# A two-pass attention and FFN kernel: the order of the first pair's units, the weight words' loads, and the way of the first unit's maxima are changed

## The reference, cut to what matters

```python
ig, fg = x @ Wi + bi, x @ Wf + bf                # x = [q, k, v], per head and token
log_f_cum = cumsum(log_sigmoid(fg))              # with a leading 0
log_D = where(ltr, log_f_cum[s] - log_f_cum[t], -inf) + ig[t]
max_log_D = max(log_D, -1)
D = exp(log_D - max_log_D)
C = (q @ k.T / sqrt(32)) * D
Cn = C / (maximum(abs(C.sum(-1)), exp(-max_log_D)) + EPS)
h = Cn @ v                                       # then normalised over the 32 features of a head
x = x + h * ln_scale
gate_up = layernorm(x) @ w_gu.T                  # fp4 values times a scale per group of 128
y = (silu(gate) * up) @ w_down.T
x = x + y / rms(y)
```

## Time and profile before

| | us |
|---|---|
| median of the runs | 559.58 |
| the profiled execution | 560.9 |
| its span | 559.2 |
| TensorE matmuls busy | 504.4 |
| VectorE busy | 391.4 |
| GpSimd busy | 331.9 |
| ScalarE busy | 295.6 |

### The profile page before, as it was taken

How to read it: one execution, slowest core, us unless ns; L and a number is a source line. 1 busy time by engine, 2 the same in 40 slices (tenths; PEclk the granted TensorE clock), 3 DMA queues, 4 the chain that set the end, 5 groups by cost and what they waited for, 6 DMA issues and landing times.

```text
span 559.2 us, 8167 instructions
## 1 busy us (share of the span) xinstructions
PE 504.4 (90%) x2728; PEld 279.4 (50%) x2728; DVE 391.4 (70%) x691; ACT 295.6 (53%) x639; POOL 331.9 (59%) x371
## 2 busy tenths in 40 slices
PE   0449989968999899999999999999999989988996
PEld 0326765425666444456665445466664443322442
DVE  4675886985888897647777899377778962877301
ACT  0335765275777623377786354577766123866000
POOL 1043533457888685466777783767777662888501
PEclk9868996988999999999999999999999999999999
DMA  8654309164200600166006000653000000200000
GB/s 254 174 156 186 114 2 320 38 227 151 77 1 2 226 1 1 42 222 240 28 2 226 1 0 4 198 212 119 2 0 2 19 20 19 94 1 1 19 20 38
DMA packets 22218, 48.33 MB, mean 86 GB/s; under 512 B 1824, under 2 KB 8864, under 8 KB 21536
## 3 DMA queue, kind: packets, MB, share of 16 engines
q1 hardware_dynamic: 22176, 47.81, 25.4%
HBM read 37.84 MB, written 4.33 MB: 75 GB/s over the span
## 4 chain that ended last, share of the span: by engine, by line
PE 68%; DVE 14%; issue 5%; ACT 4%; POOL 4%; DMA 4%; SPq 1%; DVEq 0%; POOLq 0%; ACTq 0%
PE pf L972 25%; PE pf L958 17%; PE po L896 9%; PE pq L864 6%; PE pq L876 2%; DMA ts<-in_gate_up_bytes 2%; DVE ffn L1221 2%; PE pq L958 2%; PE pq L901 2%; ACT dmat L648 2%; PE pf L981 2%; DVE ffn L1225 1%; PE pq L826 1%; POOL hT L530 1%; ACT ts L682 1%
## 5 line engine op out<-in xcount | busy, mean ns | idle before, releaser
L972 PE MATMUL pf<-w_down,hT 128*128 128x512 f32 x352 | 154.1, 595 | 1.7 <-DVE w_down L1287 1.7
L958 PE MATMUL pf<-yT,gu_val 128*128 128x512 f16 x552 | 135.6, 385 | 4.2 <-ACT th L707 1.5
L525 POOL TENSOR_TENSOR ffn<-ffn,ts 128x512 f32<-128x512 f32 x88 | 117.6, 1337 | 31.9 <-DVE ffn L1225 22.1
L682 ACT ACTIVATE ts<-pf,gu_scale 128x512 f32<-128x512 f32 x138 | 87.5, 684 | 51.1 <-PE pf L958 50.8
L972 PEld LDWEIGHTS pf<-w_down,hT 128*128 128x128 f32 x352 | 65.9, 190 | 83.7 <-issue 77.1
L958 PEld LDWEIGHTS pf<-yT,gu_val 128*128 128x128 f16 x552 | 50.7, 99 | 68.7 <-DVE ffn L1225 8.2
L648 ACT ACTIVATE dmat<-negm,aT 128x128 f32<-128x128 f32 x256 | 80.0, 395 | 4.9 <-DMA negm<-negm_dram 4.9
L530 POOL TENSOR_TENSOR hT<-ffn,th 128x512 f32<-128x512 f32 x44 | 57.6, 1313 | 30.9 <-DVE th L1234 30.9
L1221 DVE SCALAR_TENSOR_TENSOR ffn<-pf,gu_scale,ts 128x512 f32<-128x512 f32 x69 | 51.6, 748 | 33.7 <-PE pf L958 20.0
L896 PEld LDWEIGHTS po<-v_sb,dmat 128*128 128x128 f32 x512 | 64.2, 197 | 5.3 <-issue 0.9
L486 POOL TENSOR_SCALAR_AFFINE_SELECT dmat<-dmat 128x512 f32<-128x512 f32 x64 | 44.2, 704 | 30.7 <-ACT dmat L648 30.7
(11 more groups left out here) (118 smaller groups left out, 634.0 us busy)
## 6 DMA issues: line engine op xcount, KB each, us to landing
negm<-negm_dram SPq DMA_DIRECT2D x32, 512.0 KB, 5.3
ffn<-in_x SPq DMA_DIRECT2D x4, 1024.0 KB, 7.5
xT<-in_ctx_T SPq DMA_DIRECT2D x16, 256.0 KB, 5.8
ctx_sb<-in_ctx SPq DMA_DIRECT2D x4, 1024.0 KB, 5.4
x_sb<-in_x SPq DMA_DIRECT2D x4, 1024.0 KB, 5.2
x_res<-x_sb SPq DMA_DIRECT2D x4, 1024.0 KB, 5.3
out<-x_res SPq DMA_DIRECT2D x16, 256.0 KB, 2.1
ts<-in_gate_up_bytes SPq DMA_DIRECT2D x2, 704.0 KB, 11.8
```

The source lines that it names most:

```text
L525: pool.tensor_tensor(acc, acc, ts[:, h % TDEEP, 1], ALU.add).then_inc(tsum_ready, 1)
L682: act.activation(ts[:, h % TDEEP, g], bank(q, h, g), ACT.Copy, scale=gu_scale[:, g * GU + o:g * GU + o + 1]).then_inc(t_ready, 1)
L958: last = pe.matmul(bank(q, h, g), gu_val[:, h // 2 + h % 2 * FT, g], yT[:, part, g], start=(part == 0), stop=(part == 1))
L972: last = pe.matmul(pf[:, tt], hT[:, j, tt * P:(tt + 1) * P], w_down[:, j], start=(j == 0), stop=(j == FT - 1))
```

## The change

Five parts.

1. The words of the up weights are loaded in two halves, the first ahead of the context (`load_gu`), and the next pair's x is loaded already in the head, behind a wait for the transposes of x, where it stands ahead of `sc_raw`. Four chunks are decoded ahead of the gate rows and none between head and units (`UP_FIRST`, `UP_EARLY`); the statistics of the next x (`norm1_sums(1)`) take that place and leave the units.
2. The maxima of unit 0 of pair 0 are spread over the partitions by TensorE (`spread_first`, four f32 matmuls with a column of the identity), into two banks of `pf`, from where ScalarE reads them. SyncE no longer loads that unit's maxima. The turned rows go to bank 0 of `pf`. 24 fillers stand ahead.
3. In pair 0 the values of the context are centred for two tiles first, then unit 0 is masked, then the other two tiles are centred; `floors` moves behind the exponentials of unit 0.
4. In pair 0 TensorE issues both halves of the scores and the state sums of u + 1 in front of the values of u, with one group of fillers; the state sums have their own bank, and VectorE's `later_part` of a unit moves behind the products of the next.
5. In pair 1 GpSimd's mask of unit 0 stands one step earlier.

```diff
--- before
+++ after
@@ -76,8 +76,8 @@
 UP_CHUNKS = 8
-UP_FIRST = 3
-UP_EARLY = 5
+UP_FIRST = 4
+UP_EARLY = 4
 DOWN_CHUNKS = 4
@@ -213,10 +213,13 @@
         def bank_back(p):
-            return pf[:, 3] if p == 1 else pm
+            return pf[:, 0] if p == 0 else pf[:, 3] if p == 1 else pm
...
             return pf[:, 2 * half] if p == 0 and u % 2 else pq[:, 2 * half]
+        def bank_state(p):
+            return pf[:, 1] if p == 0 else pq[:, 1]
@@ -360,7 +364,8 @@
                 take_wait(sp)
-                load_units(range(1))
+                if not (isinstance(p, int) and p == 0):
+                    load_units(range(1))
@@ -401,8 +406,6 @@
                     late_negm(p)
-                    if q is None:
-                        load_xg(n, q)
                     if n is not None:
@@ -415,15 +418,23 @@
+            def load_gu(part):
+                rows = slice(part * GROW // 2, (part + 1) * GROW // 2)
+                cols = slice(part * GROW * MW // 2, (part + 1) * GROW * MW // 2)
+                for half in range(2):
+                    sp.dma_start(gu_words[half * HALF:(half + 1) * HALF, rows].rearrange("p o w -> p (o w)"),
+                                 gu_bytes[:, cols]).then_inc(s_up[part], 16)
             load_xg(0, None)
...
             sp.dma_start(bias_col[:], b_gates).then_inc(s_const, 16)
+            load_gu(0)
             load_ctxT(0)
-            for half in range(2):
-                sp.dma_start(gu_words[half * HALF:(half + 1) * HALF].rearrange("p o w -> p (o w)"), gu_bytes
-                             ).then_inc(s_up, 16)
+            load_ctx(0)
+            load_gu(1)
+            load_xg(1, None)
             sp.dma_start(sc_raw[:], gu_scales).then_inc(s_scales, 16)
-            load_ctx(0)
             for half in range(2):
@@ -464,14 +475,14 @@
-            def centre_v(p):
+            def centre_v(p, tiles=range(TT)):
                 pool.wait_ge(am_ready, 2 * p + 2)
...
                     pool.wait_ge(pv_done, UNITS * p)
-                for tt in range(TT):
+                for tt in tiles:
                     m = vmean[:, 1, tt * NH:(tt + 1) * NH].unsqueeze(2).to_broadcast([P, NH, DH])
@@ -488,7 +499,9 @@
                 hg, b = u // 2, u % 2
-                if u == 0:
+                if p == 0 and u < 2:
+                    pool.wait_ge(v_ready, 2 * u + 2)
+                elif u == 0:
                     pool.wait_ge(v_ready, TT * p + TT)
@@ -546,12 +559,12 @@
                         residual2(q - 1, TT - 1)
+                    if q == 0 and h == LATE - 1:
+                        mask(p, 0)
                     if q is not None:
...
                             gated(q, h // 2 - 1)
-                    if q == 0 and h == LATE:
-                        mask(p, 0)
                     if p is not None and slot(q, h) in MASKS:
@@ -585,8 +598,9 @@
             rstd1(0)
-            centre_v(0)
+            centre_v(0, range(2))
             mask(0, 0)
+            centre_v(0, range(2, TT))
             iteration(0, None, 1)
@@ -634,8 +648,12 @@
                 hg, b = u // 2, u % 2
+                if p == 0 and u == 0:
+                    act.wait_ge(bc_done, half + 1)
+                elif half == 0:
+                    spread = 2 * p + u // 4 + 1 - (u % 4 == 0)
+                    act.wait_ge(s_negm[u % 4], 16 * spread)
                 if half == 0:
-                    act.wait_ge(s_negm[u % 4], 32 * p + 16 * (u // 4) + 16)
                     act.wait_ge(aT_ready, p + 1)
@@ -644,8 +662,9 @@
                     bh = b * DH + hg * HG + h
+                    m = pf[:, 2 * half + 1, hh * S:(hh + 1) * S] if p == 0 and u == 0 else negm[:, u % 4, h]
                     for c in range(BLKS):
-                        last = act.activation(dmat[:, u % 2, half, c, hh], negm[:, u % 4, h, c * P:(c + 1) * P],
+                        last = act.activation(dmat[:, u % 2, half, c, hh], m[:, c * P:(c + 1) * P],
                                               ACT.Exp, bias=aT[:, c, bh:bh + 1])
@@ -781,9 +800,9 @@
             softplus(0)
-            floors(0)
             exps(0, 0, 0)
             exps(0, 0, 1)
+            floors(0)
             iteration(0, None, 1)
@@ -841,7 +860,10 @@
                 hg, b = u // 2, u % 2
-                if u == 0 and hh == 0:
+                if p == 0 and u == 1 and hh == 0:
+                    pe.wait_ge(floor_ready, 2)
+                if p > 0 and u == 0 and hh == 0:
@@ -869,11 +891,14 @@
                 pe.wait_ge(vw_ready, 2 * UNITS * p + 2 * u + 2)
-                if u > 0:
+                if p == 0:
+                    if u > 0:
+                        pe.wait_ge(state_ready, u)
+                elif u > 0:
                     pe.wait_ge(later_ready, UNITS * p + u)
...
                     pe.wait_ge(t_ready, 4 * FT * q + 2)
-                pe.matmul(pq[:, 1, 0:HG * (DH + 1)], ctx_sb[:, 2 * b, hg * P:(hg + 1) * P],
+                pe.matmul(bank_state(p)[:, 0:HG * (DH + 1)], ctx_sb[:, 2 * b, hg * P:(hg + 1) * P],
                           vw[:, u % 2].rearrange("q h d -> q (h d)"), start=True, stop=True
@@ -881,7 +906,9 @@
                     pe.wait_ge(acc_ready, 4 * FT * q + 2)
-                if u == 0:
+                if p == 0 and u < 2:
+                    pe.wait_ge(v_ready, 2 * u + 2)
+                elif u == 0:
                     pe.wait_ge(v_ready, TT * p + TT)
@@ -897,6 +924,8 @@
+                if p == 0 and u > 0:
+                    pe.wait_ge(later_ready, u)
                 pe.wait_ge(state_ready, UNITS * p + u + 1)
@@ -974,11 +1003,21 @@
-            def keep_busy(count):
+            def spread_first(half):
+                if half == 0:
+                    pe.wait_ge(nm_ready, 1)
+                for hh in range(2):
+                    r = 2 * half + hh
+                    last = pe.matmul(pf[:, 2 * half + 1, hh * S:(hh + 1) * S],
+                                     ident[0:ROWS, r:r + 1].to_broadcast([ROWS, P]), nm[:], start=True, stop=True)
+                last.then_inc(bc_done, 1)
+            def keep_busy(count, dst=None):
...
                 for _ in range(count):
-                    pe.matmul(pf[:, 3], words[:, 0:P], words.unsqueeze(1).to_broadcast([P, 2, 2 * P]),
+                    pe.matmul(pf[:, 3] if dst is None else dst, words[:, 0:P], words.unsqueeze(1).to_broadcast([P, 2, 2 * P]),
                               start=True, stop=True)
@@ -990,17 +1029,15 @@
                             scores(p, q, VALUES[s] + 1, 0)
-                            keep_busy(6 if VALUES[s] == 0 else 3)
+                            state_sums(p, q, VALUES[s] + 1)
+                            scores(p, q, VALUES[s] + 1, 1)
+                            keep_busy(6, po[:]) if VALUES[s] == 0 else keep_busy(3)
                         if s in VALUES:
                             values(p, q, VALUES[s])
-                            if q is None and VALUES[s] + 1 < UNITS:
-                                scores(p, q, VALUES[s] + 1, 1)
-                                state_sums(p, q, VALUES[s] + 1)
-                                keep_busy(6 if VALUES[s] == 0 else 3)
                         if s in SCORES and (q is not None or SCORES[s] == 0):
...
                             if q is None:
-                                keep_busy(16)
+                                keep_busy(8, po[:])
                             state_sums(p, q, SCORES[s])
@@ -1027,7 +1064,10 @@
             gate_sums(0)
+            keep_busy(24, po[:])
+            spread_first(0)
             turn_back(0)
+            spread_first(1)
             iteration(0, None, 1)
@@ -1128,7 +1168,7 @@
                 dve.wait_ge(st_done, UNITS * p + u + 1)
-                dve.tensor_tensor(state[:, u % 2], pq[:, 1, 0:HG * (DH + 1)].rearrange(
+                dve.tensor_tensor(state[:, u % 2], bank_state(p)[:, 0:HG * (DH + 1)].rearrange(
                     "q (h d) -> q h d", h=HG), own_rows[:], ALU.mult).then_inc(state_ready, 1)
@@ -1265,7 +1305,9 @@
                     dve.wait_ge(const_ready, 7)
-                    dve.wait_ge(s_up, 32)
+                    dve.wait_ge(s_up[0], 32)
+                if i == UP_CHUNKS // 2:
+                    dve.wait_ge(s_up[1], 32)
                 r = slice(i // 2 * QROW, (i // 2 + 1) * QROW)
@@ -1294,6 +1336,10 @@
                         keep_state(p, u)
+                        if u > 0:
+                            later_part(p, u - 1)
+                    if q is None and s - 1 in VALUES and VALUES[s - 1] == UNITS - 1:
+                        later_part(p, UNITS - 1)
                     if q is not None:
@@ -1303,13 +1349,11 @@
                         decode_up(i) if i < UP_CHUNKS else decode_down(i - UP_CHUNKS)
-                    if p is not None and s in VALUES:
+                    if p is not None and q is not None and s in VALUES:
                         later_part(p, VALUES[s])
...
                         add_later(p, ADD[s])
```

(10 more changed lines are left out.)

## The result

Measured were 589.37 us (587.04 to 589.58, 4 runs) against 559.12 us before in the same session: a ratio of 1.0539, 95% interval 1.0475 to 1.0603. The forecast was 589. The profiled execution after has a span of 587.6 us and a mean granted clock of 0.922; before it was 0.967.

What follows compares the result with a forecast made beforehand. TensorE was taken to bound the kernel, busy 424.14 of 443.50 us after 115.7. Head 48.7, rounds 67.2 and unit 7 4.6 gave 120.5 against 88.57, +31.9; less 2.2, +29.7: 590.6, at the median 589, range 568 to 596.

Steps and rivals of the forecast that it cites:

- the stage: First pair's head, six rounds and unit 7 together: end of unit 7's values at 120.5 against 88.57, +31.9 us.
- the second pair: Start of the second pair: earlier mask removes TensorE's wait for `vw` before the state sums, -2.2 us, bounds 0 and -3.
- The 1.3 taken off at the end: Whole-kernel time: profiled execution before lay 1.3 us above the median of its runs, so 590.6 makes 589.
- The ring: First pair: values of u wait via `vw` and exponentials for values of u-1; 11.2 us a round, six rounds 67.2.
- The clock: TensorE in the six first-pair rounds: low level, 1.2 GHz, for all six; chance 0.65.
- The head: Before the rounds: `nm` ready at 29.5, but unit 0's values end at 48.7 us, against 47.23 before.
- the 0.8 for it: In the head: `sc_raw`, queued later and read ahead of the softplus, costs 0 to 2 us, taken as 0.8.
- Unit 7: Last unit of the first pair: values need only unit 6's copy, 4.6 us instead of 7.43.
- Rival (a): First-pair rounds: ring closes but the clock stays up, 8.1 to 8.2 us a round, 566 in all; chance 0.09.
- Rival (c): First-pair rounds: TensorE stays the bound, a unit loses one filler group, 4.4 us a round, 546 in all; chance 0.02.

Runs made afterwards that it cites:

- the order alone: Kernel before with only part 4: score halves and state sums of u+1 ahead of the values of u, own bank, later part moved; 595.3 us, ratio 1.0645.
- three buffers: Changed kernel with three `dmat` buffers, not two; first-pair exponentials of u+1 wait for values of u-2 and precede the copy of u-1; 570.25 us, ratio 1.0185.
- The moved mask alone: Kernel before with only part 5, GpSimd's first mask of the second pair behind one sum instead of three; 554.26 us against 559.05, ratio 0.9924.
- the old round put back: Changed kernel with TensorE's first-pair round ordered as before (second score half and state sums behind the values, two filler groups), all else kept; 548.61 us, ratio 0.9802.
- the profiled execution with six fillers: Changed kernel with three `dmat` buffers, opened exponentials and six fillers per unit instead of three; profiled at 562.44 us, median 561.5 of ten runs.
- the one entered at the high clock: Kernel with three buffers and six fillers per unit, plus 14 fillers once ahead of unit 1's state sums; profiled at 551.27 us, four runs 549.22 to 560.51.

## Why the prediction was right

The mechanism, the sign and the size were right; that 589 and 589.37 lie within half a microsecond is luck. By the two traces the kernel became 28.4 us longer (587.6 - 559.2), by the sum 29.7: the stage gave +32.1 against 31.9, the second pair -3.7 against -2.2. The 1.3 taken off at the end, because the profiled execution before lay above its median, made up for that: the one after lay at its median (589.29).

- **The ring** is right, in its edges and in its size. From the end of the values to `vw` it was priced at 4.2 and took 4.07 (47.96 to 52.03), TensorE's part at 7.0 and took 7.2; a round 11.2 against 11.33, six rounds 67.2 against 68.0. The 0.2 on TensorE are the scores and the state sums: the scores' half takes 1.16 from start to start at the low clock (52.82 to 53.98), where I took 1.03 from a row in which the clock was coming back, and the state sums 0.73 instead of 0.58. That the exponentials close it is shown by opening them (no wait, 8.29), that the order alone does it by the order alone (595.3).
- **The clock** was taken as low for all six rounds, and it was 0.50 from 48 to 116 us. The level was right, the reason is shown only in part. I put it down mainly to the idle time. For it: in the order alone the clock fell with the first stall, and with fillers in the stall it was 1.00. Against it as the only cause: with three buffers and no wait it was 0.52. The row that I leaned on, the gap of 0.82 us in front of 82.60, was also one outcome of two. The moved mask alone leaves the first pair as it was, and in its execution the same gap of 0.82 (in front of 78.52) was followed by state sums in 0.46 and three fillers in 0.81, the high level. The Trainium skill, "TensorE: Matmul & The Clock Gate", section "HAM oscillation — how this bites in real kernels", tells of a loop whose burst of matmuls is shorter than the wait behind it and is throttled again in every turn. The 0.50 of the rounds agrees in direction, but this ring is not that case, as its burst of 8.4 us is longer than its stall of 2.97; and three buffers had the low clock with no wait at all. So the chance of 0.65 for the low clock in all six rounds rested on weaker ground than it seemed.
- **The head** was right in its sum, 48.7 forecast and 47.96 measured, by terms that were partly off and made up for one another, which is luck too. The words were there in time and four chunks ended at 21.98 (22.2). `sc_raw` was read at 22.68, ahead of the softplus at 24.26: the 0.8 for it was nothing. The gate sums took 5.42 us instead of 3.66 and held the gate rows until 23.30; the old round put back has the same head and took 3.66, so that belongs to the execution and not to the change. So the gate rows began 1.8 us earlier than before and not 2.1, and `nm` was ready at 29.82 (29.5). Two spreading matmuls took 0.97 us (I took 1.8), but a load of ScalarE's table, 1.28 us, came between `aT` and the exponentials, which I had not priced:

```profile
31.68 1.28 ACT L667 ACT_TABLE_LOAD   x1 [5.27 <-DVE aT L1156]
32.97 2.17 ACT L667 ACTIVATE dmat<-pf,aT 128x128 f32<-128x128 f32 x8
...
35.94 2.45 ACT L667 ACTIVATE dmat<-negm,aT 128x128 f32<-128x128 f32 x8 [0.60 <-DMA negm<-negm_dram]
```

  The maxima of unit 1 landed 3.9 us after their issue at 32.01, not 5.1; the queue had one load less, but that this is the reason is not shown. `vw` of unit 1 was ready at 40.16 (40.5). The state sums of unit 1 then waited for something that I had not on the path, VectorE's `keep_state` of unit 0, which empties their bank and ended at 40.42:

```profile
40.57 0.46 PE L901 MATMUL pf<-vw,ctx_sb 128*128 128x132 f32 x2 [1.78 <-DVE state L1171]
```

  It cost some 0.4 us here (40.16 to 40.57). From there to the end of the values it took 7.39 us and not 8.3, because state sums (0.46) and scores (0.71) still ran at the high level; from 42 to 48 us the clock was 0.50.
- **Unit 7** took 4.70 (4.6), and its values ended at 120.67 (120.5).
- **The second pair** is the term that was mis-sized most: -2.2 forecast for the wait, -3.7 measured. The step that failed is "-2.2, bounds 0 and -3": it counted the wait and not the fall of the clock behind it, 1.41 in the next eight matmuls and 0.31 in the values. The rows were there in the trace before, 3.31 at 129.95 and 2.18 at 133.06. The moved mask alone confirms it, with 2.7 to 5.7 us less.
- Rival (a) was what fillers in the wait made of the kernel: 8.03 a round at the high clock, forecast 8.1 to 8.2. Rival (c) is refuted by the wait for `vw` in each round; its own sum, by the way, gives 545 and not 546.

## What to carry to other kernels

Before moving a consumer in front of work on an engine that issues in order, follow what it waits for back through the other engines; if that comes round to the work it was moved ahead of, or to the same work one turn earlier, an overlap has become a ring, and its length is the sum of all its parts. The slack is read from the trace beforehand: here `vw` came 4.98 us after the values and was asked for at 5.70. And filler matmuls taken away as waste can be what holds the clock (with the state sums behind the values, three fillers lost it and took 8.13 us a round, six kept it and took 5.06): price a move at both clock levels, and count the fall of the clock behind a wait with the wait.

## What the runs showed of the hardware that I had not expected

TensorE can be recorded as busy all the time and still be granted half the clock: 48.50 of 48.50 us busy at 0.52 with three f16 fillers of 512 columns in a unit, 40.00 of 40.00 at 0.74 with six, and 35.00 of 35.00 at 1.00 in the old round, also with six, but in two groups. The same matmuls in a round took 6.8 us in the profiled execution with six fillers and 5.12 in the one entered at the high clock, and run times near both levels occur for either kernel. What decides between them was not settled. The ends of matmuls are modelled in the trace, so short gaps may hide in this busy time. The Trainium skill, same page, section "A second HAM failure mode: psum-queue depth-cycling", tells of a kernel whose clock swings between its levels because TensorE idles briefly between groups of matmuls; the swing is seen here (six fillers in 2.74 us, scores in 0.71), such gaps are not.
